# Two cross-attention layers on one core: one averaging product for the statistics and the scores' bias, fixed PSUM banks for the small products, and three reorderings

## What is computed

```python
# layer 0, per batch of 32: x, y are 128 x 1024
q, k = Wq @ y + bq, Wk @ y + bk                 # 128 channels, 8 heads of 16
v = Wv @ x + bv
attn = softmax(q_h @ k_h.T / sqrt(128))         # per head, 16 x 16
o = Wo @ concat(attn_h @ v_h) + bo + x
h = (o - mean(o)) * rsqrt(var(o) + eps) * gn_w + gn_b    # over the whole 128 x 1024

# layer 1, per batch: h and y as 128 tokens x 1024
q = lora(h, Wq, Aq, Bq)                         # 32 heads of 32
k, v = lora(y, Wk, ...), lora(y, Wv, ...)       # 8 key/value heads
out = h + lora(softmax(q @ k.T / sqrt(32)) @ v, Wo, Ao, Bo)
```

## Time and profile before

| what | value |
|---|---|
| runs | 1291.48 us median, 1291.04 to 1292.23 |
| profiled execution, own time | 1291.69 us |
| its span (first to last instruction) | 1290.1 us |
| TensorE busy | 1273.8 us, 99% |
| VectorE busy | 875.5 us, 68% |
| ScalarE busy | 816.3 us, 63% |
| GpSimd busy | 150.3 us, 12% |
| granted TensorE clock | 1.00 in all stages |
| DMA | 318.66 MB, mean 247 GB/s |
| chain that ended last | TensorE 94%, DMA 2%, VectorE 2% |

### The profile page before, as it was taken

The page is one execution under the profiler, slowest core; times in us unless marked ns, Lnnn a source line. Parts: engine busy times, 40 slices in busy tenths (PEclk is TensorE's granted clock), DMA queues, the critical chain, the costliest instruction groups (busy, mean ns, idle before and its releaser), DMA issues.

```text
span 1290.1 us, 22770 instructions
## 1 busy us (share of the span) xinstructions
PE 1273.8 (99%) x6836; PEld 1023.4 (79%) x6836; DVE 875.5 (68%) x2005; ACT 816.3 (63%) x2884; POOL 150.3 (12%) x117
## 2 busy tenths in 40 slices
PE   8999999999999999999999999999999999999998
PEld 6788888888888888888888888777776777777676
DVE  6777667777757777777777775786665666666554
ACT  6676766666506777777667776766665666654440
POOL 4344443222200000000000003200000000000000
PEclk9999999999999999999999999999999999999999
DMA  9688889898758877777777889999999999988872
GB/s 315 223 271 279 270 264 307 297 299 293 241 185 244 230 228 229 229 234 231 222 206 226 235 223 301 260 258 253 266 258 256 244 263 257 273 233 236 233 227 82
DMA packets 191783, 318.66 MB, mean 247 GB/s; under 512 B 21136, under 2 KB 85904, under 8 KB 190960
## 3 DMA queue, kind: packets, MB, share of 16 engines
q1 hardware_dynamic: 191664, 317.22, 84.1%
HBM read 232.20 MB, written 84.93 MB: 246 GB/s over the span
## 4 chain that ended last, share of the span: by engine, by line
PE 94%; DMA 2%; DVE 2%; SPq 1%; issue 1%; ACT 0%; DVEq 0%
PE bank L670 27%; PE bank L703 23%; PE bank L551 13%; PE bank L725 8%; PE bank L758 5%; PE bank L773 5%; PE bank L623 3%; PE bank L536 2%; PE bank L641 2%; DMA lora_raw_q<-in_factors_q 1%; PE bank L656 1%; PE bank L578 1%; PE bank L595 1%; PE bank L525 1%; PE bank L602 1%
## 5 line engine op out<-in xcount | busy, mean ns | idle before, releaser
L992 ACT ACTIVATE bank<-bank,negs 128x128 f32<-128x128 f32 x1024 | 348.6, 343 | 175.3 <-DVE negs L1263 175.1
L670 PE MATMUL bank<-hT,wq 128*128 128x512 f32 x1488 | 390.3, 400 | 0.0
L703 PE MATMUL bank<-wo,op 128*128 128x512 f32 (+1 forms) x1356 | 346.9, 393 | 0.8 <-DVE h_blk L1357 0.8
L670 PEld LDWEIGHTS bank<-hT,wq 128*128 128x128 f32 x1488 | 264.0, 189 | 46.2
L703 PEld LDWEIGHTS bank<-wo,op 128*128 128x128 f32 x1356 | 249.6, 189 | 54.8 <-DVE op L1315 1.6
L1258 DVE TENSOR_REDUCE maxes<-bank 128x4 f32<-128x512 f32 x256 | 175.6, 686 | 151.2 <-PE bank L725 151.1
L1013 ACT ACTIVATE probT<-bank 128x512 f32<-128x512 f32 x256 | 151.0, 608 | 138.0 <-PE bank L758 132.8
L992 ACT ACTIVATION_READ_ACCUMULATOR bank<-bank,negs 128x1 f32 x1024 | 211.9, 207 | 0.0
L551 PE MATMUL bank<-wkv_hi,yT 128*128 128x512 f32 x512 | 206.0, 421 | 0.7 <-POOL wkv_lo L1513 0.6
L725 PEld LDWEIGHTS bank<-k_stack,q_stack 96*128 96x128 f32 x1024 | 150.3, 191 | 17.3 <-issue 1.5
L725 PE MATMUL bank<-k_stack,q_stack 96*128 96x128 f32 x1024 | 147.2, 266 | 1.2 <-DMA q_stack<-q_dram 1.2
(11 more groups left out here) (141 smaller groups left out, 1482.7 us busy)
## 6 DMA issues: line engine op xcount, KB each, us to landing
q_stack<-q_dram SPq DMA_DIRECT2D x256, 256.0 KB, 4.0
q_dram<-q_part SPq DMA_DIRECT2D x64, 512.0 KB, 4.1
q_stack<-q_dram SPq DMA_DIRECT2D x256, 128.0 KB, 4.5
yT_in<-in_ctx_turned SPq DMA_DIRECT2D x32, 512.0 KB, 4.6
y_in<-in_ctx SPq DMA_DIRECT2D x32, 512.0 KB, 6.9
x_in<-in_x SPq DMA_DIRECT2D x32, 512.0 KB, 5.7
h_dram<-h_out SPq DMA_DIRECT2D x32, 512.0 KB, 7.7
h_in<-h_dram SPq DMA_DIRECT2D x32, 512.0 KB, 3.6
```

Source lines behind the costliest of these rows:

```text
L670: m = pe.matmul(bank(u % 2).rearrange("p (a n) -> p a n", a=2), wq[:, block, part, c, :], hT[(group + 1) % 2][:, :, of, c, :], start=c == ...
L703: mm = pe.matmul(place[:, columns], op_of(pair, m)[:, of, c, :], wo[m][w][:, c, columns], start=fresh and c == 0 and of == 0 and w == 0, s ...
L992: act.activation(part, part, ACT.Exp, bias=negs[:, n % RING, j:j + 1], scale=SCORE1, accum_out=sums[:, score_column(k), g, j:j + 1]).then_ ...
```

## The change

1. The second score product (L585) and `s_bq` go. Instead ScalarE scales Wk.T by the sum of y (`scale_keys`: once in full into `y_keys`, once rounded to fp32r), GpSimd subtracts for the lower part (`lower_keys`), and the averaging product multiplies those 2 x 128 columns along with the 2 x 2 columns of the statistics. The average over partitions of Wk.T times the sum of y, times 128 and bq, is the bias of the scores. VectorE adds it in two operations (`bias_scores`) before the scores come.
2. The averaging product is fp32r: the statistics are split in two parts by VectorE in `partition_stats`, and `deviation` sums the two results (`stat_sums`). For batches 0 and 1 the bias has a product of its own (`bias_product`). For the last two there is no bias part.
3. Bank 6 is for the chain gram, t1, s, n1, mix; bank 7 for units, statistics and bias. Each weights' unit of the loop is made one batch later, right behind the Gram products, and merged behind `evacuate_t1`. Unit 38 is made after the loop, in bank 6.
4. `stats_product` goes behind K/V chunk 6, `var_product` behind chunk 7. On VectorE, `rest_mix` goes ahead of `deviation`, and that ahead of `norm_factors`.
5. The loads of the first two sets of score keys go from slot 20 to slot 10 of SP's list (`FIRST_KEYS`).
6. In the last pair of the output stage, `add_out` 0 and 1 go ahead of `split_op` 3 and behind `split_op` 4.
7. The first load loses the 128 columns of bq; `mix` shares the tile of `n1`.

```diff
+        def use_small(bank_number, key, freed_by):
+            small[key] = bank(bank_number)
+            if bank_number in last_use:
+                small_freed[key] = last_use[bank_number]
+            last_use[bank_number] = freed_by
         for b in range(B):
-            small_uses += [(("gram", b), "gram", b + 1), (("t1", b), "t1", b + 1), (("s", b), "s_sb", b + 1),
-                           (("n1", b), "n1", b + 1), (("mix", b), "xbias", b + 1)]
+            if b > 1:
+                use_small(7, ("prep", unit_of(b - 1)), ("prep_merged", unit_of(b - 1) + 1))
+            for name, done in (("gram", "gram"), ("t1", "t1"), ("s", "s_sb"), ("n1", "n1"), ("mix", "xbias")):
+                use_small(6, (name, b), (done, b + 1))
+            if b < 2:
+                use_small(7, ("u", b), ("u_bias", b + 1))
             if b:
-                small_uses += [(("st", b - 1), "nm", b), (("prep", unit_of(b)), "prep_merged", unit_of(b) + 1)]
+                use_small(7, ("st", b - 1), ("u_bias", b + 2) if b + 1 < B else ("st_sum", b))
...
+        use_small(6, ("kT", B - 1), ("kT", B))
...
+        for n in (N_UNITS - 2, N_UNITS - 1):
+            use_small(6, ("prep", n), ("prep_merged", n + 1))
...
+        FIRST_KEYS = 10
...
-                score_keys_at.setdefault(max(soonest, score_slot[n - 5] + 1) if n >= 8 else soonest, []).append(n // GQ)
+                score_keys_at.setdefault(max(soonest, score_slot[n - 5] + 1) if n >= 8 else FIRST_KEYS, []).append(n // GQ)
```

TensorE:

```diff
             def stats_product(b):
-                pe.wait_ge(S["st"], b + 1)
-                pe.wait_ge(S["st2"], b)
-                pe.matmul(ps[:, 0:2], ones_avg[:], both_st, start=True, stop=True).then_inc(S["st1_mm"], 1)
+                of = slice(0, 2 + P if b + 2 < B else 2)
+                pe.wait_ge(S["st_lo"], b + 1)
+                if b + 2 < B:
+                    pe.wait_ge(S["u_lo"], b + 3)
+                pe.matmul(averages(ps, of), ones_avg[:], averaged[:, :, of], start=True, stop=True).then_inc(S["st1_mm"], 1)
...
-                pe.matmul(ps[:, 0:P], wqT0, t1[:], start=True, stop=False)
-                pe.wait_ge(S["sbq"], b + 1)
-                pe.matmul(ps[:, 0:P], s_bq[:], wkT0, start=False, stop=True).then_inc(S["s_mm"], 1)
+                pe.matmul(ps[:, 0:P], wqT0, t1[:], start=True, stop=True).then_inc(S["s_mm"], 1)
...
             for b in range(1, B):
                 gram_products(b)
+                if b > 1:
+                    prep_product(unit_of(b - 1))
                 kv_products(b, (0,))
...
                 mix_product(b)
-                stats_product(b - 1)
                 kv_products(b, (6,))
-                prep_product(unit_of(b))
+                stats_product(b - 1)
                 if last:
                     turn_h(2)
+                kv_products(b, (7,))
                 if b - 1 >= LATE_STATS:
                     var_product(b - 1)
-                kv_products(b, (7,))
...
             mixed_x(B - 1)
             turn_k(B - 1)
+            prep_product(N_UNITS - 2)
```

ScalarE and GpSimd:

```diff
-                act.activation(s_bq[:], bqk[:, 0, :], ACT.Copy, scale=y_sum[:, b % 2:b % 2 + 1]).then_inc(S["sbq"], 1)
+                act.wait_ge(S["ysum"], b + 1)
+                if b:
+                    act.wait_ge(S["u_lo"], b)
+                act.activation(y_keys[:], wkT0, ACT.Copy, scale=y_sum[:, b % 2:b % 2 + 1]).then_inc(S["u_full"], 1)
...
+                act.activation(averaged[:, 0, 2:2 + P], wkT0, ACT.Copy,
+                               scale=y_sum[:, b % 2:b % 2 + 1]).then_inc(S["u_hi"], 1)
...
                 begin_gram(b)
-                scale_bias(b)
...
                 sum_y(b + 1)
+                scale_keys(b + 1)
                 evacuate_n1(b)
...
+            def lower_keys(b):
+                pool.wait_ge(S["u_full"], b + 1)
+                pool.wait_ge(S["u_hi"], b + 1)
+                pool.tensor_tensor(averaged[:, 1, 2:2 + P], y_keys[:], f32(averaged[:, 0, 2:2 + P]),
+                                   ALU.subtract).then_inc(S["u_lo"], 1)
...
             for b in range(1, B):
+                lower_keys(b + 1)
                 if 0 <= b - 2 < LATE_STATS:
                     power(b - 2)
                 lower_x(b)
```

VectorE:

```diff
             def partition_stats(b):
...
+                dve.tensor_scalar(averaged[:, 0, 0:2], both_st, 1.0, None, ALU.mult).then_inc(S["st_hi"], 1)
+                dve.wait_ge(S["st_hi"], b + 1)
+                dve.tensor_tensor(averaged[:, 1, 0:2], both_st, f32(averaged[:, 0, 0:2]), ALU.subtract).then_inc(
+                    S["st_lo"], 1)
             def deviation(b):
...
+                dve.tensor_reduce(stat_sums[:], averages(small["st", b], slice(0, 2)).rearrange("p a n -> p n a"), AX_X,
+                                  ALU.add).then_inc(S["st_sum"], 1)
...
+            def bias_scores(b):
...
+                dve.scalar_tensor_tensor(att[:], lower, bq_scaled[:, 1:2], score_bias[:], ALU.mult, ALU.add).then_inc(
+                    S["u_low"], 1)
+                dve.wait_ge(S["u_low"], b + 1)
+                dve.scalar_tensor_tensor(att[:], upper, bq_scaled[:, 1:2], att[:], ALU.mult, ALU.add).then_inc(
+                    S["u_bias"], 1)
...
                 evacuate_t1(b)
+                if b > 1:
+                    prep_merge(unit_of(b - 1))
...
                 add_mix(b)
                 rest_yT(b + 1, 1)
-                if 0 <= b - 2 < LATE_STATS:
-                    norm_factors(b - 2)
-                deviation(b - 1)
                 if last:
                     split_hT(1)
                 rest_mix(b)
+                deviation(b - 1)
+                if 0 <= b - 2 < LATE_STATS:
+                    norm_factors(b - 2)
+                bias_scores(b + 1)
                 if 0 <= b - 2 < LATE_STATS:
                     norm_scale(b - 2)
                 if b - 1 >= LATE_STATS:
                     norm_factors(b - 1)
-                prep_merge(unit_of(b))
...
+                    final = pair == PAIRS - 1
                     if i == 1:
                         combine(pair, 3)
+                        if final:
+                            add_out(pair, 0)
                         split_op(pair, 3)
                     if i == 2:
-                        add_out(pair, 0)
+                        if not final:
+                            add_out(pair, 0)
                         split_op(pair, 4)
+                        if final:
+                            add_out(pair, 1)
```

More of the change, by code:

```diff
@@ L101, in xattn_two_layers @@
         factor_tiles(lora, "lora", F32R, "kv", "o")
-        ones_avg = sb("ones_avg", [P, P])
-        first = sb("first", [P, 6 * P + 5])
-        w0T, wv0, bqk = first[:, 0:3 * P], first[:, 3 * P:4 * P], first[:, 4 * P:6 * P].rearrange("p (a n) -> p a n", a=2)
+        ones_avg = sb("ones_avg", [P, P], F32R)
+        first = sb("first", [P, 5 * P + 5])
+        w0T, wv0, bk_row = first[:, 0:3 * P], first[:, 3 * P:4 * P], first[:, 4 * P:5 * P]
         score_bias = sb("score_bias", [P, P])
-        bq_col, bv_col, bo_col, gnw_col, gnb_col = (first[:, 6 * P + i:6 * P + i + 1] for i in range(5))
-        bq_scaled = sb("bq_scaled", [P, 1])
+        bq_col, bv_col, bo_col, gnw_col, gnb_col = (first[:, 5 * P + i:5 * P + i + 1] for i in range(5))
+        bq_scaled = sb("bq_scaled", [P, 2])
         minus_half = sb("minus_half", [P, 1])
@@ L112, in xattn_two_layers @@
         t1 = sb("t1", [P, P])
-        s_bq = sb("s_bq", [P, P])
+        y_keys = sb("y_keys", [P, P])
+        averaged = sb("averaged", [P, 2, 2 + P], F32R)
+        stat_sums = sb("stat_sums", [P, 2])
         att = sb("att", [P, P])
         n1 = sb("n1", [P, P])
-        mix = sb("mix", [P, P])
+        mix = n1
         mix_split = sb("mix_split", [P, 2, P], F32R)
@@ L571, in var_product @@
                 pe.wait_ge(S["st2"], b + 1)
-                pe.matmul(ps[:, 0:1], ones_avg[:], st2, start=True, stop=True).then_inc(S["st2_mm"], 1)
+                pe.matmul(ps[:, 0:1], f32(ones_avg[:]), st2, start=True, stop=True).then_inc(S["st2_mm"], 1)
             def t1_product(b):
@@ L810, in tensor_program @@
                 score_product(b)
+                if b == 1:
+                    bias_product(1)
                 mixed_x(b - 1)
@@ L1180, in norm_scale @@
                 dve.tensor_scalar(gbi[b % 2], nm[b % 2], gsc[b % 2], gnb_col, ALU.mult, ALU.add).then_inc(S["gbi"], 1)
-            def softmax0_begin(b):
+            def bias_scores(b):
+                if b >= B:
+                    return
+                upper, lower = (averages(small["st", b - 2] if b >= 2 else small["u", b], slice(2, 2 + P))[:, part, :]
+                                for part in range(2))
                 if b:
@@ L1376, in vector_program @@
             dve.wait_ge(S["first_in"], DMA)
-            dve.tensor_scalar(bq_scaled[:], bq_col, SCORE0 * L, None, ALU.mult).then_inc(S["bq_scaled"], 1)
-            dve.wait_ge(S["bq_scaled"], 1)
```

(9 more changed lines are left out.)

82 lines of the change are left out of this document (58 added, 24 removed).

## The result

The changed kernel takes **1309.32 us** (median of 4 runs, 1307.76 to 1310.11), the kernel before 1291.26 beside it: ratio 1.0124, 95% interval [1.0105, 1.0143]. The profiled execution took 1310.11 us with a span of 1308.5 and a mean granted clock of 0.996 (before: 1290.1). The forecast was 1283.7 with a range up to 1288.8, and 0.07 for slower. It was wrong in sign.

What follows compares the result with a forecast made beforehand. TensorE, busy 99% of the span, was taken as the bound. From 1291.6 us, periods -8.3, last batches -0.2, head +0.6, stage change +1.7, keys -0.6, last pair -1.1 gave -7.9: 1283.7 us, range 1280.0 to 1288.8.

Steps and rivals of the forecast that it cites:

- VectorE, per batch: VectorE's added and moved operations in each batch keep part of TensorE's gain: -0.30 us a batch, -8.3 over 28 periods.
- (c): TensorE, each batch: the weights' unit ahead of the first K/V chunk covers its wait for ScalarE's copy, -0.11 us.
- the ring over VectorE: Batch loop: VectorE's tail, scalings and Gram sums, no longer TensorE alone, set the period, 9.95 us a batch.
- the slower one: Batch loop: GpSimd's lower-keys subtraction blocks VectorE up to 0.45 us a batch, period 10.4, 1296.2 us; chance 7%.
- (a): TensorE, each batch: the second score product, two fp32 passes of 128 columns, goes, -0.22 us.
- (b): TensorE, each batch: the averaging product becomes one fp32r product of 260 columns, 0.12 us instead of 0.22, -0.10.
- ScalarE: Each batch: two scalings ahead of the n1 copy make it some 0.07 us late, and the mix product waits.
- the first rival: Batch loop: TensorE stays the bound, the period falls by 0.36 to 0.43 us, time 1281.1 us; chance 18%.
- Head: Batch 1, nothing yet in step: extra VectorE work, less a smaller first load, +0.6 us (-0.3 to +1.8).
- Last two batches: End of the batch loop, with other work in the places of the changed operations: -0.2 us.
- Stage change: Behind the loop: unit 38 waits for VectorE to read the keys, last mixed product later, +1.7 us (+0.6 to +2.5).
- Keys: Query stage: earlier key loads shorten the first score product's 1.25 us wait for its queries, -0.6 us.

Runs made afterwards that it cites:

- experiment 5: Kernel before the change, with only fixed banks 6 and 7 and the weights' unit a batch later behind the Gram products: 1288.93 us, ratio 0.9974.
- experiment 9: Changed kernel with the weights' unit behind K/V chunk 1, rest_mix back behind the deviation, and unit 38 a step later in the query stage: 1283.51 us, ratio 0.9922.
- experiment 1: Changed kernel with the weights' unit behind K/V chunk 1 instead of right behind the Gram products: 1290.86 us, ratio 0.9995.
- Experiment 7: Changed kernel with the weights' unit behind K/V chunk 1 and rest_mix back behind the deviation: 1285.95 us, ratio 0.9936.
- experiment 2: Changed kernel with the bias operations ahead of the deviation and bank 7 freed by the statistics' sum: 1312.03 us, ratio 1.0144.
- Experiment 6: Kernel before the change, with only the first score keys loaded at slot 10 and the last pair's sums earlier: 1292.51 us, ratio 0.9986.

## Why the prediction was wrong

**The step that failed** is in "VectorE, per batch": "The two bias operations fit into the time of the power." So they do, and VectorE loses nothing by them. But I asked only what they delay on their own engine, not who waits for what they read. They are the last readers of bank 7, and paragraph (c) put the unit, which writes bank 7, at 0.95 us into the batch. My own numbers were enough: the variance's first step stands 0.6 into the next batch, some 0.1 later the bias begins, and two of 0.3 end it at 1.3. By these numbers the unit would start 0.35 us behind its due time; it started 0.63 behind it. The diff says it in one line, `use_small(7, ("st", b - 1), ("u_bias", b + 2) ...)`, and I quoted it. The unit and the chunk behind it (229.82 to 230.87, 1.05 us) then entered the ring over VectorE through the turn that the second Gram sum needs, and the period went to 10.57 instead of 9.95: a step forecast at -0.30 us came out at +0.32, and over all 28 with their four long ones +11.0 us where -8.3 was forecast. None of the four rivals held this mechanism; the slower one (GpSimd shuts VectorE out, 1296.2) was another and did not come true: the lower keys' subtraction ran at 226.05 to 226.46 while VectorE was at operations with one input, as argued.

The Trainium skill's *Perfetto Trace Analysis*, section "Matmuls", says that independent groups should rotate through different PSUM banks so that the evacuation of one overlaps the next group's matmuls. The traces agree as far as this: the unit went into the bank whose evacuation ended last (1.52 us into the batch) and stood for it. That the two banks no longer rotate over the seven small groups of a batch isn't the fault by itself: experiment 5 has them fixed, and its step is 10.13, less than the 10.25 with rotation.

Step by step:

- **(a), (b)** right: no row for the second score product; the averaging product takes 0.12, as taken from the Gram products of the same type.
- **(c)** right in size (0.12 by experiment 5), wrong in the change, where the bank is shut. The reading "0.70 elsewhere" was too wide: in the trace of the kernel before the chunk behind the statistics' product (156.83) takes 0.81 as well, and experiment 9 still has such a chunk (0.80).
- **ScalarE** near enough: the copy of n1 comes late behind the two scalings, and in experiment 9 the mix product takes 0.30 us in the chain; but it took 0.27 before, so this is +0.03 for +0.07. **GpSimd** right in the loop.
- **The ring over VectorE** right in kind: 10.02 measured in experiment 1 against 9.95. Its unit stands elsewhere, so whether the 0.07 is in my four short operations or in that place stays open. Experiment 7 shows that one operation put back, rest_mix, which I had priced at 0.2 and left ahead of the variance, is what made the ring bind: without it 9.87, or 0.38 off. That lies in the first rival's 0.36 to 0.43 by luck, since it is made up otherwise: in the chain of experiment 9 the second score product is gone (-0.22), the averaging product shorter (-0.10), t1 no longer waits (0.30 to 0.22), the mix product is late (+0.03), and (c) gives nothing.
- **Head** mis-sized: +1.4 for +0.6. The row of 1.62 us at 32.86 is not the operation with two SBUF inputs that I priced, but the rounding ahead of it, with one. What lies above the forecast is the failed step again: the moved unit waits 0.68 there, and without that wait the head costs +0.4 (experiment 9).
- **Last two batches** mis-sized: +0.7 for -0.2; the variance's product waits 1.41 us for the bias operations, one more reader of bank 7 that I didn't ask about.
- **Stage change** right: the wait before unit 38 was 0.98 for 1.1, and with the clock whole the stretch costs 53.6 - 52.05 = +1.5 for +1.7. The slow clock that came on top in the first profiled execution, 2.6 us, I had not thought of.
- **Keys**: all of the 1.25, where I took the middle. **Last pair**: right, 1.2 for 1.1.

Experiment 9, which has the averaging product without the unit's wait, and rest_mix and unit 38 elsewhere, shows what the change can give once three pieces are moved: span 1280.7, 9.4 us less than before. That its time of 1283.5 is nearly the forecast's 1283.7 is luck: it is another kernel with other terms, and beside it the kernel before took 1293.0, so it is 9.5 us less where 7.9 less was forecast. These are, by its own trace: head +0.4, 28 periods -7.0 (280.09 against 287.12; the early batches are up to 2 us longer than the median), last batch +0.6, stage change 0, keys -1.25, first scores to the last products -1.0 (inside the spread told above), last products -1.2.

## What to carry to other kernels

Whenever an instruction is moved to an earlier place on its engine, look up the last reader of the buffer that it writes and put that reader's end, in microseconds into the loop, beside the new due time; an operation that "fits into a gap" is free for its own engine only, and keeps its input shut until it is done. Count such a wait from the due time and not by the bracket: here the bracket said 0.48 us, the unit was 0.63 late, and moving it brought back 0.55. Moving the reader ahead only handed the wait on (experiment 2); moving the writer back by a chunk that was there anyway removed it.

## What the runs showed of the hardware

**The same gaps do and don't cost the clock.** After waits of 1.41, 1.18 and 0.40 us the granted clock fell to 0.50 (1.2 GHz) for 3 to 7 us in three executions and stayed at 1.00 in four; the changed kernel alone did both. (Experiment 2's clock fell from 351 to 354 us too, behind a wait of 1.45.) The loop of the kernel before does both as well. Experiment 6 has its batch loop unaltered and the same waits of 1.22 and 1.15 us in the head, yet TensorE's timeline there reads

```profile
34.84 0.80 PE L526 MATMUL bank<-lora_q 96*128 96x512 f32 x1 [1.15 <-DVE norm L1206]
...
36.72 1.91 PE L537 MATMUL bank<-yT 128*128 128x256 f32 x8
```

The kernel before took 0.50 and 1.11 us for these two rows, and 12.99 us from the turn of batch 1 to that of batch 2 where experiment 6 took 15.12: 2.1 us between two executions of the same code. One profile with a slow stretch is no evidence for the edit that it is compared with; I had taken it for that.

**A scaling with one SBUF input can be shut out by GpSimd.** Besides the 1.62 us in the head, the last scaling of the softmax (L1272) takes 0.29 us as a rule, and in two of the four long batches this, in the timeline of GpSimd and VectorE:

```profile
53.02 1.30 POOL L1600 TENSOR_TENSOR wq<-w_raw,wq 128x512 fp32r<-128x512 f32 x1
...
53.31 1.10 DVE L1272 TENSOR_SCALAR att<-att,att_stat 128x128 f32<-128x128 f32 x1
```

It ends at 54.41, GpSimd's operation at 54.32; the row of 1.62 us in the head ends at 34.48, GpSimd's at 34.46. In the prediction I looked for this only in operations with two inputs. The Trainium skill, *SBUF — State Buffer*, "Who interferes with whom", says that `tensor_scalar` too can take the shared port pair in a two-port mode, and that the one that comes second is blocked for the whole of the other's instruction. These two rows agree; no run here tried the operation in a form without that mode.
